# A state scan with its state in 32x32 blocks, and its matrix products on the diagonal of the array

## What is computed

```python
def step(state, inp):                      # state: (batch, head, 16, 16)
    q_t, k_t, v_t, a_t, b_t = inp
    state = a_t[..., None, None] * state
    stored = jnp.einsum('bhij,bhj->bhi', state, k_t)
    delta = b_t[..., None] * (v_t - stored)
    state = state + jnp.einsum('bhi,bhj->bhij', delta, k_t)
    o_t = jnp.einsum('bhij,bhj->bhi', state, q_t)
    return (state, o_t)
_, outs = jax.lax.scan(step, state0, (qT, kT, vT, aT, bT))
```

## Time and profile before

| | |
|---|---|
| time, median of 3 runs | 4116.24 us (4115.43 to 4116.9) |
| profiled execution, its own time | 4122.16 us |
| its span | 4120.4 us |
| state scan in the span | about 925 to 1435 us |
| TensorE clock granted in the scan | 0.50 |

### The profile page before, as it was taken

How to read it: one execution, slowest core, us unless ns; L and a number is a source line. 1 busy time by engine, 2 the same in 40 slices (tenths; PEclk the granted TensorE clock), 3 DMA queues, 4 the chain that set the end, 5 groups by cost and what they waited for, 6 DMA issues and landing times. The chain is left out here.

```text
span 4120.4 us, 91537 instructions
## 1 busy us (share of the span) xinstructions
PE 2660.1 (65%) x34356; PEld 1875.9 (46%) x34356; DVE 2279.7 (55%) x5471; ACT 1246.8 (30%) x3021; POOL 539.6 (13%) x613
## 2 busy tenths in 40 slices
PE   5986876238888746554666468777882019999800
PEld 2554544235555523332333346555562019999700
DVE  2485656725666568886611457667766014444466
ACT  3664553225666501111300034334431002222200
POOL 0221211000000001110000001001010650000065
PEclk8997877555555578887776589888895559999955
DMA  2536465663333284402097632121211422222255
GB/s 99 188 126 241 159 249 181 239 215 97 104 100 102 89 208 124 123 20 84 21 399 299 240 145 68 54 67 54 68 50 48 164 90 71 70 70 71 83 167 178
DMA packets 413008, 538.32 MB, mean 131 GB/s; under 512 B 178932, under 2 KB 341712, under 8 KB 403408
## 3 DMA queue, kind: packets, MB, share of 16 engines
q1 hardware_dynamic: 361840, 381.38, 28.8%
q0 software_dynamic: 39616, 127.22, 8.5%
q10 hardware_dynamic: 11296, 26.22, 1.6%
HBM read 329.68 MB, written 216.15 MB: 132 GB/s over the span
## 5 line engine op out<-in xcount | busy, mean ns | idle before, releaser
L1021 ACT ACTIVATE ss_write_ps<-ss_state,ss_gammas 128x64 f32<-128x64 f32 x1024 | 263.3, 302 | 195.6 <-DVE ss_state L1069 195.6
L443 PE MATMUL dc_rows_ps<-dc_weights,dc_hT 128*128 128x512 f32 x512 | 291.3, 698 | 8.5 <-issue 4.8
L1193 PE MATMUL do_late_ps<-do_scratch,do_ident 128*128 128x512 f32 (+1 forms) x416 | 197.2, 632 | 109.7 <-DVE do_scratch L1228 109.7
L2546 PE MATMUL se_up_ps<-se_xT,se_w 128*128 128x128 f32 x2176 | 267.5, 277 | 0.1
L500 PE MATMUL dc_solve_ps<-dc_sides,dc_blocks 32*32 32x32 f32 x8192 | 123.4, 226 | 215.0 <-ACT dc_blocks L594 99.0
L2554 PE MATMUL se_y_ps<-se_w,se_aT 128*128 128x256 f32 x1088 | 257.2, 380 | 0.0
L2546 PEld LDWEIGHTS se_up_ps<-se_xT,se_w 128*128 128x128 f32 x2176 | 255.9, 193 | 0.5 <-DVE se_w L2611 0.5
L2611 DVE COPY se_w<-mx_weights 128x2048 f32 x136 | 166.7, 1227 | 100.4 <-issue 100.4
L2682 POOL DMA_INDIRECT cb_y<-scratch_ys,cb_to x128 | 137.6, 1075 | 593.0 <-DVE cb_to L2697 554.6
L500 PEld LDWEIGHTS dc_solve_ps<-dc_sides,dc_blocks 32*32 32x32 f32 x8192 | 110.8, 138 | 228.5 <-ACT dc_blocks L594 119.0
L2554 PEld LDWEIGHTS se_y_ps<-se_w,se_aT 128*128 128x128 f32 x1088 | 196.6, 191 | 20.9
(11 more groups left out here) (346 smaller groups left out, 5650.1 us busy)
## 6 DMA issues: line engine op xcount, KB each, us to landing
ex_w<-in_w_all SPq DMA_DIRECT2D x64, 1024.0 KB, 21.2
scratch_rows<-dc_rows POOLq DMA_DIRECT2D x64, 512.0 KB, 4.2
scratch_vw<-dc_out POOLq DMA_DIRECT2D x64, 512.0 KB, 4.5
dc_c_rows<-scratch_rows SPq DMA_DIRECT2D x64, 384.0 KB, 4.6
scratch_xs<-wa_zeros ACTq DMA_DIRECT2D x34, 512.0 KB, 13.5
se_xs<-scratch_xs SPq DMA_DIRECT2D x136, 128.0 KB, 2.1
scratch_ys<-se_y SPq DMA_DIRECT2D x136, 128.0 KB, 1.7
ss_wq_rows<-scratch_vw SPq DMA_DIRECT2D x128, 128.0 KB, 2.2
```

Source lines behind the costliest of these rows:

```text
L443: mm = pe.matmul(to, hT[n % 2][:, k, :], weights[:, k, columns], start=(k == 0), stop=(k == HALVES - 1), skip_group_check=True)
L1021: ins = act.activation(write_ps[b][:, k, 0:WIDTH], state[b][:, k, :], ACT.Copy, scale=gammas[i][:, b, k, c:c + 1])
L1193: mm = pe.matmul(late_ps[:, to:to + (2 - skip) * DIM], ident[:, :], scratch[lag % 2][:, (t + skip - lag) * DIM:(t + 2 - lag) * DIM], start ...
L2546: mm = pe.matmul(up_ps[i % 2][:, c * P:(c + 1) * P], w[i % (2 * AHEAD)][:, k * DFF + c * P:k * DFF + (c + 1) * P], xT[i % 2][:, k, :], sta ...
```

## The change

The state of two heads is kept as one 32x32 block. The 128 partitions are four groups of 32 (`group_of(u)`), and each has two blocks side by side (`columns_of(s)`): the state is 128 x 2 x 32 in place of 128 x 2 x 64. Reads and writes are one product for each block, eight for a sequence instead of four, each of them 32 weight columns by 32 columns; the read has 32 partitions. The decay and the mask work on the smaller state. `wq` has no zeros and isn't cleared. For the order of heads that this needs, `wq_rows` are loaded by halves with rows of 32 elements, eight loads for a tile where there were four; the mask is loaded in four pieces; the decays are laid out in that order in the first stage; and `unit_column` changes. TensorE's loop over pairs of tiles is now a Python loop: its instructions are written out for all 32 tiles. The other engines keep their hardware loops.

```diff
-    return (u % HALVES) * P + (u // HALVES) * WIDTH
+    return u * WIDTH
...
+def slot_columns(rows, s):
+    return rows.rearrange("p (u s e) -> p u s e", u=UNITS, s=HALVES)[:, :, s, :]
...
-                    seq_b.tell(vec.tensor_copy(last[:, :, :], spread(sm(GAMMA)[:, T - 1, :], HEAD)), last_ready, g + 1)
+                    for s in range(HALVES):
+                        heads = sm(GAMMA)[:, T - 1, :].rearrange("p (u s j) -> p u s j", u=UNITS, s=HALVES)[:, :, s, :]
+                        copy = vec.tensor_copy(last[:, s * HEADS // HALVES:(s + 1) * HEADS // HALVES, :].rearrange("p (u j) e -> p u j e", u=UNITS), spread(heads, HEAD))
...
-        state = [sb(f"state{b}", [P, HALVES, WIDTH]) for b in range(BATCH)]
+        state = [sb(f"state{b}", [P, HALVES, BLOCK]) for b in range(BATCH)]
...
+        def blocks():
+            for s in range(SIDES):
+                for u in range(UNITS):
+                    yield u, s
...
-                sync.dma_start(block_mask[:, :], d["block_mask"]).then_inc(consts, 16)
-                sync.wait_ge(cleared, at(4))
+                for g in range(P // BLOCK):
+                    sync.dma_start(block_mask[g * BLOCK:(g + 1) * BLOCK, :], d["block_mask"][g * BLOCK:(g + 1) * BLOCK, columns_of(g % SIDES)]).then_inc(consts, 16)
+                sync.wait_ge(cleared, at(2))
...
-                        sync.dma_start(wq_rows[i][:, b, 0, :], vw_v[b, bass.ds(tile, 1), :, DIM:2 * DIM].rearrange("a p f -> (a p) f")).then_inc(wq_in[i], 16)
-                        sync.dma_start(wq_rows[i][:, b, 1, :], vw_v[b, bass.ds(tile, 1), :, 3 * DIM:4 * DIM].rearrange("a p f -> (a p) f")).then_inc(wq_in[i], 16)
+                        for n in range(2):
+                            rows = vw_v[b, bass.ds(tile, 1), :, (2 * n + 1) * DIM:(2 * n + 2) * DIM].rearrange("a p f -> (a p) f")
+                            for s in range(SIDES):
+                                sync.dma_start(wq_rows[i][:, b, n, s * P:(s + 1) * P].rearrange("p (u e) -> p u e", u=UNITS), slot_columns(rows, s)).then_inc(wq_in[i], 16)
...
-                                for u in range(UNITS):
-                                    k = u % HALVES
-                                    mm = pe.matmul(read_ps[b][u * QUAD:(u + 1) * QUAD, 0:WIDTH], wq[i][:, b, u, c, :], state[b][:, k, :], start=True, stop=True, skip_group_check=True)
+                                for u, s in blocks():
+                                    mm = pe.matmul(read_ps[b][u * QUAD:(u + 1) * QUAD, columns_of(s)], wq[i][group_of(u), b, s, c, :], state[b][group_of(u), s, :], start=True, stop=True, skip_group_check=True)
...
-                                for u in range(UNITS):
-                                    k = u % HALVES
-                                    mm = pe.matmul(write_ps[b][side_of(u), k, 0:WIDTH], k_rows[i][rows_of(u), b, c, :], solved[i][rows_of(u), b, c, :], start=False, stop=True, skip_group_check=True)
+                                for u, s in blocks():
+                                    mm = pe.matmul(write_ps[b][group_of(u), s, 0:BLOCK], k_rows[i][rows_of(u), b, c, columns_of(s)], solved[i][rows_of(u), b, c, columns_of(s)], start=False, stop=True, skip_group_check=True)
...
-                with pe.Fori(0, PAIR - 1) as ii:
-                    tile_pair(ii, more=True)
-                tile_pair(PAIR - 1, more=False)
+                for ii in range(PAIR):
+                    tile_pair(ii, more=ii + 1 < PAIR)
...
-                                    ins = act.activation(write_ps[b][:, k, 0:WIDTH], state[b][:, k, :], ACT.Copy, scale=gammas[i][:, b, k, c:c + 1])
+                                    ins = act.activation(write_ps[b][:, k, 0:BLOCK], state[b][:, k, :], ACT.Copy, scale=gammas[i][:, b, k, c:c + 1])
...
-                    vec.memset(wq[i][:, :, :, :, :], 0.0).then_inc(cleared, 1)
...
-                                vec.tensor_tensor(state[b][:, :, :], write_ps[b][:, :, 0:WIDTH],
-                                                  block_mask[:, :].unsqueeze(1).broadcast_to([P, HALVES, WIDTH]), ALU.mult).then_inc(state_ready[b], 1)
+                                vec.tensor_tensor(state[b][:, :, :], write_ps[b][:, :, 0:BLOCK],
+                                                  block_mask[:, :].unsqueeze(1).broadcast_to([P, HALVES, BLOCK]), ALU.mult).then_inc(state_ready[b], 1)
```

More of the change, by code:

```diff
@@ L757, in decays @@
                         vec.wait_ge(last_turned, at(g))
-                    seq_b.tell(vec.tensor_copy(last[:, :, :], spread(sm(GAMMA)[:, T - 1, :], HEAD)), last_ready, g + 1)
+                    for s in range(HALVES):
+                        heads = sm(GAMMA)[:, T - 1, :].rearrange("p (u s j) -> p u s j", u=UNITS, s=HALVES)[:, :, s, :]
+                        copy = vec.tensor_copy(last[:, s * HEADS // HALVES:(s + 1) * HEADS // HALVES, :].rearrange("p (u j) e -> p u j e", u=UNITS), spread(heads, HEAD))
+                        if s == 0:
+                            seq_b.done(copy)
+                    seq_b.tell(copy, last_ready, g + 1)
                 def factors(g):
@@ L854, in build_state_scan @@
     N = TILE_CHUNKS
+    BLOCK = 2 * HEAD
+    SIDES = WIDTH // BLOCK
     with ExitStack() as ctx:
@@ L860, in build_state_scan @@
         ident = sb("ident", [P, P])
-        block_mask = sb("block_mask", [P, WIDTH])
+        block_mask = sb("block_mask", [P, BLOCK])
         wq_rows = [sb(f"wq_rows{i}", [P, BATCH, 2, DIM]) for i in both]
@@ L865, in build_state_scan @@
         solved = [sb(f"solved{i}", [P, BATCH, N, WIDTH]) for i in both]
-        wq = [sb(f"wq{i}", [P, BATCH, UNITS, N, 2 * CHUNK]) for i in both]
+        wq = [sb(f"wq{i}", [P, BATCH, HALVES, N, 2 * CHUNK]) for i in both]
         gammas = [sb(f"gammas{i}", [P, BATCH, HALVES, N]) for i in both]
-        state = [sb(f"state{b}", [P, HALVES, WIDTH]) for b in range(BATCH)]
+        state = [sb(f"state{b}", [P, HALVES, BLOCK]) for b in range(BATCH)]
         turn_ps = [ps(f"turn_ps{i}", [P, HALVES, 2 * P]) for i in both]
@@ L886, in build_state_scan @@
         PAIR = BATCH_TILES // 2
-        WQ_LOADS = 2 * BATCH * 16
+        WQ_LOADS = 2 * BATCH * SIDES * 16
         LOADS = 2 * UNITS * BATCH * 16
@@ L891, in build_state_scan @@
         SETS = BATCH * 2
+        CONSTS = (1 + P // BLOCK) * 16
         TURN_AT, COPY_AT, TAKE_AT = 1, 2, 7
@@ L896, in rows_of, with group_of, columns_of @@
             return slice(u * QUAD, u * QUAD + CHUNK)
-        def side_of(u):
-            return slice(u // HALVES * WIDTH, (u // HALVES + 1) * WIDTH)
+        def group_of(u):
+            return slice(u * BLOCK, (u + 1) * BLOCK)
+        def columns_of(s):
+            return slice(s * BLOCK, (s + 1) * BLOCK)
+        def blocks():
+            for s in range(SIDES):
+                for u in range(UNITS):
+                    yield u, s
         sem.start()
@@ L952, in _ @@
             def _(pe):
-                pe.wait_ge(consts, at(32))
+                pe.wait_ge(consts, at(CONSTS))
                 def turn(tile, i, pair, n, k):
@@ L959, in turn @@
                     if n >= 2 and k == 0:
-                        pe.wait_ge(wq_low, at(tile * SETS + n - 1))
-                        pe.wait_ge(wq_high, at(tile * SETS + n - 1))
+                        pe.wait_ge(wq_first, at(tile * SETS + n - 1))
+                        pe.wait_ge(wq_second, at(tile * SETS + n - 1))
                     mm = pe.transpose(turn_ps[n % 2][:, k, 0:P], wq_rows[i][:, n // 2, n % 2, k * P:(k + 1) * P], ident[:, :])
@@ L968, in tile_pair @@
                         tile = ii * 2 + i
-                        pe.wait_ge(wq_low, at((tile + 1) * SETS))
-                        pe.wait_ge(wq_high, at((tile + 1) * SETS))
+                        pe.wait_ge(wq_first, at((tile + 1) * SETS))
+                        pe.wait_ge(wq_second, at((tile + 1) * SETS))
                         for c in range(N):
@@ L994, in _ @@
                     for k in range(HALVES):
-                        mm = pe.matmul(write_ps[b][:, k, 0:WIDTH], ident[:, :], state[b][:, k, :], start=True, stop=True, skip_group_check=True)
+                        mm = pe.matmul(write_ps[b][:, k, 0:BLOCK], ident[:, :], state[b][:, k, :], start=True, stop=True, skip_group_check=True)
                 mm.then_inc(primed, 1)
@@ L1008, in copy_turned @@
                     act.wait_ge(turned, at(tile * SETS + n + 1))
-                    act.copy(wq[i][side_of(0), n // 2, 0:HALVES, :, n % 2 * CHUNK:(n % 2 + 1) * CHUNK],
-                             turn_ps[n % 2][side_of(0), :, 0:P].rearrange("p k (c t) -> p k c t", c=N)).then_inc(wq_low, 1)
+                    act.copy(wq[i][0:WIDTH, n // 2, :, :, n % 2 * CHUNK:(n % 2 + 1) * CHUNK],
+                             turn_ps[n % 2][0:WIDTH, :, 0:P].rearrange("p k (c t) -> p k c t", c=N)).then_inc(wq_first, 1)
                 def tile_pair(ii, more):
```

9 lines of the change are left out of this document (4 added, 5 removed).

## The result

The changed kernel takes 4205.59 us (median of 3 runs, 4202.45 to 4208.62) against 4116.24 before: ratio 1.0222, 95% interval 1.0209 to 1.0236. It is slower by 89 us, where 54 were forecast. Its profiled execution took 4202.45 us, the span 4200.6.

The account below looks back on a forecast made before the run. A chain of waits bounded the scan; SyncE's queue, held by code fetches, would set 17.3 us a tile. +3, +57, -4 and -2 make +54 on 4122, 4176, and 6 less against the runs' median: 4170 us, range 4095 to 4205.

Parts of the forecast that it names:

- The chain: Scan: a plain step saves 0.17 us, a tile goes from 15.4 to 14.4 us, the stage loses 32 us.
- rival D: Scan: matmuls start no closer than L977's 23 ns; 2.3 us more a tile, 4187 us; chance 0.03.
- Fetches: Scan, TensorE's loop written out: 1060 instructions a tile, 4.15 packets of 16 KB, 3.5 us apart at the densest.
- SyncE's queue: Scan: four more loads, and issues held by fetches; 13.6 + 3.7 = 17.3 us a tile, which sets the tile.
- TensorE's own stalls: Scan: instructions come just as fast as needed, 14.5 against 14.4 us; tile taken as 14.4 to 15.4 with stalls.
- Rival B: Scan: SyncE isn't held long, TensorE waits for instructions; 14.5 to 16.6 us a tile, 4087 to 4155 us; chance 0.17.
- The sign that I named: Scan: TensorE standing at "issue" for much over 0.5 us a tile would show the prediction wrong.
- second limit over two tiles: Scan: issue to landed store, then 14.4 us to the tile's end; 33.5 us for two, 16.8 each, not binding.
- Rival C: Scan: packets at 1.1 us each and loads at 0.61, or stalls on top; beyond 4205 us; chance 0.05.
- Rival A: Scan: a packet holds no SyncE issue; tile 14.4 to 14.7 us, time 4082 to 4092 us; chance 0.12.
- Small parts: Ahead of the scan: no wq clearing, more mask and wq loads, -2 us together; decay copies and outputs stage 0.

Follow-up runs that it names:

- The shortened bodies: Looped changed kernel with constants and GpSimd's loads, fewer matmuls in each pair's second tile: 1,880, 1,630, 1,240 instructions took 4192.82, 4080.50, 4056.81 us.

## Why the forecast fell short

*The chain*: right in kind, 14.4 forecast, 14.8 measured without fetches. A step without a turn falls from 1.77 to 1.64 (1.61 forecast); bursts are as dense as forecast, (0.65 - 0.239) / 31 = 13.3 ns from matmul to matmul for 32 of them. The change's own gain is 0.6 us a tile, some 20 us, not 32. The floor of rival D (about 25 ns, the Trainium skill, "TensorE: Matmul & The Clock Gate", Part 1) is not there.

*Fetches*: 4.15 forecast, 4.0 to 4.1 found; spacing at the least 3.3 to 3.4 us in the kernels with straight code, 3.5 forecast.

*SyncE's queue*, the term that the sum goes by: 17.3 forecast, 18.05 measured. It is 13.5 of issues and stores (13.2 forecast), 3.9 of holds (3.7; 3.9 / 4.0 = 0.98 us a packet in place of 0.90) and 0.6 between blocks (0.4; the loop's jump was taken for a gap between two issues). Right in kind, and 0.75 us too small: 22 us in 30 tiles, of the 36 by which the time exceeds the forecast. SyncE still had a wait in 9 of 23 tiles, at most 1.4 us: nearly, not wholly, the never-catching-up that was forecast.

*The step that failed*, apart from this size, is the sum's treatment of TensorE's own stalls, "I take 14.4 to 15.4 with these stalls". I compared the rate of packets with the rate of code: 4.15 x 3.5 = 14.5, just enough. What counts is the time from a packet's start until its code runs, 2.6 us, against the time that the instructions left at that moment last, 1.5 us. Measured without SyncE in the way, TensorE's tile is 17.6 us, 2.8 above the chain, where I allowed at most 1.0. It was to lie at least 1.9 us below SyncE's, and lies 0.5 below. Rival B, "fetching alone bounds", would by itself have meant 4171 us and not its 4087 to 4155. The sign that I named, TensorE at "issue" for much over 0.5 us a tile, came: 1.0 us a tile in breaks of over 0.52 us, outside the waits for a store.

*And the two don't hide each other wholly*. I took the longer of the two, 17.3 over 15.4. Measured, 18.05 for SyncE and 17.6 for TensorE make 18.3. The "second limit over two tiles" was said not to bind at 16.8, with 14.4 for the tile behind the store. With the stalls of its later steps (from its first mask to its last it is 14.6 us on the mean and 13.0 at the least, so 1.6) that tile is about 16.3 at most, and with 2.5 for the landing the limit is (17.4 + 2.5 + 16.3) / 2 = 18.1, as long as SyncE's own sum. Which of the two holds in a given tile isn't shown; that the stores' place made no difference speaks for SyncE's sum.

Per tile: -0.6 chain, +2.8 TensorE out of code, +0.7 SyncE on top, 2.9 together; 30 tiles are 87 of the 89 us. These shares are differences between kernels, and they hold for that order of removal: the 0.7 is what freeing SyncE gives back while code still stalls. In the changed kernel's own trace the larger part has the other name: VectorE's waits for a store are 51.8 / 22.6 = 2.3 us a tile, TensorE's breaks outside them 1.0. SyncE's 3.9 us of holds, which make its queue late, come with the fetches as TensorE's breaks do. By the numbers above SyncE would need about 18.05 - 3.9 = 14.2 us a tile without them, an estimate; no run has SyncE's eight loads, all of the work and no fetches.

*The range* ended at 4205, 0.6 us below what was measured. That it came so near is in part luck, since it had neither the stalls nor the size of SyncE's queue right. Its ends, 4138 and 4205, aren't what its bounds add up to either: 16.3 and 18.8 us a tile give 4140 and 4215. Rival C had what happened in three words, "stalls on top", at 0.05, beside a price of 1.1 us a packet that did not occur. (Rival A's upper end adds up to 4090 or 4091, not 4092; nothing hangs on it.)

*Small parts*: the scan starts 5 us earlier, 2 forecast.

No kernel here beats the one before with the whole work in it. The chain without fetches promises at most 0.6 us a tile, and needs a pair of tiles in some 1,630 instructions, where its 32-column products alone need 2,048. A loop over single tiles, which would have to pick `wq` and `k_rows` by a register, was not tried.

## What to carry to other kernels

Count the instructions of a tile before splitting matmuls: twice as many smaller ones can shorten every step and still lose, because the code has to arrive as well. To price straight code, compare the time from a fetch's start until its code runs with how long the instructions still at hand last, not the two mean rates. When two waits of nearly one length sit in the same tile, removing either gives back only the difference; free each one alone before giving either the whole loss. And before adding up idle times of two engines, lay them side by side in the timeline: 50 us of TensorE's "issue" were VectorE's wait for a store.

## What the runs showed of the hardware that I had not expected

- A loop's code stays on TensorE at about 1,630 instructions (104 KB, with 255 of them to a packet of 16 KB, or 64 B each) and is fetched anew in every pass at about 1,880 (120 KB), where TensorE stands for 3.5 to 4.0 us at each jump back. At 2,140 that is about 5.2 us, and the loop is slower than straight code (4241.6 against 4218.3 us). The shortened bodies are one run each, with the fetches counted in the trace.
- Where TensorE stalls, the fetch of 16 KB started when about 107 instructions were left, and its code ran 2.5 to 2.6 us later, whether the loads beside it had 4,096 or 1,024 small pieces a tile.
- An issue of SyncE's that meets a fetch ends late: 0.32 us becomes 1.2 to 1.6, 0.98 us a packet over the changed kernel's scan, although the code is TensorE's.
- Straight code costs nothing that the time shows where it is run slowly enough: 57 fetches in 415 us, 1.0002 (0.9991 to 1.0013).
- Semaphores cleared on TensorE one behind the other start 117 ns apart: eight take 0.87 us, of which 0.44 lengthened the step.
